# Expert products W1 and W2 from fp16 parts, the weights split on GpSimd during the attention, token rows stored as parts, silu over a whole tile

## What is computed

```python
t = x.reshape(4096, 192); n = layernorm(t)
gate = n @ Wg.T + bg                    # 8 experts
idx = argmax(gate)                      # top 1, so its probability is 1
h = silu(n @ W1[idx].T) * (n @ W2[idx].T)      # W1, W2: 469 x 192
out = t + h @ W3[idx].T                        # W3: 192 x 469
```

## Time and profile before

| | us |
|---|---|
| median of 3 runs | 1055.98 (1052.8 to 1056.65) |
| the profiled execution, its own time | 1051.83 |
| its span, first to last instruction | 1050.0 |
| PE busy | 944.2 |
| DVE busy | 698.3 |
| ACT busy | 631.4 |
| POOL busy | 182.6 |

### The profile page before, as it was taken

How to read it: one execution, slowest core, us unless ns; L and a number is a source line. 1 busy time by engine, 2 the same in 40 slices (tenths; PEclk the granted TensorE clock), 3 DMA queues, 4 the chain that set the end, 5 groups by cost and what they waited for, 6 DMA issues and landing times. The chain is left out here.

```text
span 1050.0 us, 26495 instructions
## 1 busy us (share of the span) xinstructions
PE 944.2 (90%) x8360; PEld 526.3 (50%) x8360; DVE 698.3 (67%) x1074; ACT 631.4 (60%) x1260; POOL 182.6 (17%) x324
## 2 busy tenths in 40 slices
PE   3799958999999999999999999977482999999995
PEld 1566622333333333333333333376481787878784
DVE  6664558999999999999999999335326344434341
ACT  3564416888888888888888888842112343434441
POOL 3340000000000000000000000050301344444442
PEclk9897757999999999999999999987555999999998
DMA  5244762333333333333333332079520111111110
GB/s 148 76 117 161 286 221 60 101 97 96 101 86 98 91 99 94 96 99 89 99 88 99 94 98 80 2 214 240 149 68 19 40 47 52 49 47 57 54 35 2
DMA packets 75791, 101.08 MB, mean 96 GB/s; under 512 B 27747, under 2 KB 44626, under 8 KB 74214
## 3 DMA queue, kind: packets, MB, share of 16 engines
q1 hardware_dynamic: 65012, 80.13, 27.0%
q0 software_dynamic: 10288, 19.76, 6.8%
q10 hardware_dynamic: 450, 0.66, 0.2%
HBM read 72.25 MB, written 30.05 MB: 97 GB/s over the span
## 5 line engine op out<-in xcount | busy, mean ns | idle before, releaser
L804 DVE TENSOR_REDUCE neg_max<-max_ps 128x1 f16<-128x1024 f32 x384 | 452.3, 1222 | 47.0 <-PE max_ps L658 46.5
L787 ACT ACTIVATE probs<-ring_ps 128x512 f32<-128x512 f32 x768 | 413.3, 595 | 64.9 <-PE ring_ps L690 63.4
L690 PE MATMUL ring_ps<-q_side,k_side 113*128 113x512 f16 x768 | 234.1, 386 | 2.0 <-ACT probs L787 1.6
L702 PE MATMUL out_ps<-probs,values 128*32 128x256 f32 x3072 | 205.6, 385 | 0.1
L702 PEld LDWEIGHTS out_ps<-probs,values 128*32 128x32 f32 x3072 | 80.4, 109 | 109.9 <-ACT probs L787 56.2
L658 PE MATMUL max_ps<-k_side,q_side 48*128 48x256 f16 x1536 | 122.8, 279 | 13.4 <-ACT ident L762 7.2
L1383 DVE TENSOR_TENSOR hidden<-hid_ps,silu 118x128 f32<-118x128 f32 (+1 forms) x156 | 45.2, 290 | 108.3 <-ACT silu L1349 108.3
L1349 ACT ACTIVATE silu<-hid_ps 118x128 f32<-118x128 f32 (+1 forms) x156 | 42.5, 273 | 107.7 <-PE hid_ps L1292 107.7
L658 PEld LDWEIGHTS max_ps<-k_side,q_side 48*128 48x128 f16 x1536 | 49.7, 95 | 113.0 <-issue 65.8
L1289 PE MATMUL hid_ps<-slot_t,w_top 128*118 128x128 f32 (+1 forms) x624 | 102.7, 288 | 0.6 <-ACT slot_t L1330 0.6
L690 PEld LDWEIGHTS ring_ps<-q_side,k_side 113*128 113x128 f16 x768 | 51.7, 97 | 99.8 <-ACT probs L787 71.8
(11 more groups left out here) (178 smaller groups left out, 933.1 us busy)
## 6 DMA issues: line engine op xcount, KB each, us to landing
q_side<-rel_split SPq DMA_DIRECT2D x384, 64.0 KB, 2.1
q_side<-qk_split SPq DMA_DIRECT2D x192, 64.0 KB, 2.4
rel_split<-rel_hi SPq DMA_DIRECT2D x6, 1024.0 KB, 4.3
rel_split<-rel_lo SPq DMA_DIRECT2D x6, 1024.0 KB, 6.3
q_side<-qk_split SPq DMA_DIRECT2D x48, 128.0 KB, 2.7
k_side<-qk_split SPq DMA_DIRECT2D x144, 32.0 KB, 1.7
w_top_all<-in_w_t POOLq DMA_DIRECT2D x2, 1876.0 KB, 19.1
qk_split<-att_sb SPq DMA_DIRECT2D x24, 128.0 KB, 2.4
```

Of the source, the lines that this page charges most:

```text
L690: nc.tensor.matmul(ring_ps[turn_of(k) % BANKS][:], k_side[slot(s)][:, tile * P:(tile + 1) * P], q_side[slot(s)][:, tile // 2, (i % 2) * HA ...
L702: last = nc.tensor.matmul(out_ps[quarter * 2 * HD:(quarter + 1) * 2 * HD, :], values[j][:, tile, :], probs[:, u % 2 * GROUP + 2 * i + quar ...
L787: nc.scalar.activation(probs[:, u % 2 * GROUP + i, :], ring_ps[turn_of(k) % BANKS][:], ACT.Exp).then_inc(exp_done, 1)
L804: nc.vector.tensor_reduce(neg_max[:, j % 2, t:t + 1], max_ps[t % 2][:], AX, ALU.max, negate=True).then_inc(tile_max, 1)
```

## The change

- W1, W2 and the normalized tokens are held as two float16 parts, a high one and the rest. In `experts` each product is five fp16 matmuls for each chunk (high x high, high x rest and rest x high for 128 channels; for the other 64, both weight parts against the tokens' high and low part, the tail standing twice in the row), 40 per tile. W3 stays float32.
- PE's step is now: all four chunks with W1, `transposes(n+1)` (four in fp16), all four chunks with W2, `output(n-1)`.
- ACT takes one silu over 512 columns, DVE one product over 512 columns. ACT copies no weights any more; DVE copies `w_top` (1888 fp16 numbers) and `w_tail` (944) first in its step and W3's part last. POOL's program in `experts` is as it was.
- POOL splits the weights in `attention`: four loads before step 0, then a copy and a subtraction in each of steps 3 to 18 (tails), two loads in step 19, a copy and a subtraction in each of steps 24 to 39 (tops). The loop over 48 steps is written out. `load_experts` in `gate` loads W3 only. The position tiles of `project` lie in the buffer that takes the weights afterwards.
- In `gate`, ACT makes the tokens' high part, DVE the rest, POOL doubles the tails, and SP stores 1024 bytes per token in one DMA for each group in place of 768 and 256 in two. The clearing of `slot_rows` moves there from `project`.

The diff, cut:

```diff
-            nc.gpsimd.memset(g.slot_rows[:], 0.0).then_inc(rows_zeroed, 1)
-            pool.wait_ge(rows_zeroed, 1)
...
-            steps(pool, BH, SLOTS, step)
+            done = [0]
+            def split_step(instruction):
+                done[0] += 1
+                instruction.then_inc(split, 1)
+                pool.wait_ge(split, done[0])
+            def split_tail(c):
+                whole = g.weights[:, c * FP:c * FP + F]
+                split_step(nc.gpsimd.tensor_copy(g.w_tail[:, c, 0:F], whole))
+                split_step(nc.gpsimd.tensor_tensor(g.w_tail[TAIL:2 * TAIL, c, 0:F], whole[TAIL:2 * TAIL, :], g.w_tail[TAIL:2 * TAIL, c, 0:F], ALU.subtract))
+            def split_top(c):
+                whole = g.weights[:, (c + 1) * FP:(c + 1) * FP + F]
+                split_step(nc.gpsimd.tensor_copy(g.w_top[:, c, 0, 0:F], whole))
+                split_step(nc.gpsimd.tensor_tensor(g.w_top[:, c, 1, 0:F], whole, g.w_top[:, c, 0, 0:F], ALU.subtract))
+            by_channel = [w.rearrange("e k f -> k e f") for w in (g.w1_t, g.w2_t)]
+            TAILS_FROM, TOPS_FROM = 3, 24
+            for part in range(2):
+                for j in range(2):
+                    pool.wait_ge(g.rel_stored[part][j], 16 * (HEADS // 4))
+            staged = lambda first: g.weights[:, first * FP:(first + 2 * EXPERTS) * FP].rearrange("p (e h f) -> p h e f", h=2, f=FP)[:, :, :, 0:F]
+            for h in range(2):
+                for half in range(2):
+                    pool.dma_start(staged(0)[half * TAIL:(half + 1) * TAIL, h], by_channel[h][P:D]).then_inc(tails_loaded, 16)
+            for n in range(BH):
+                step(Step(n, n // SLOTS, n % SLOTS, BH, True))
+                if n == TAILS_FROM:
+                    pool.wait_ge(tails_loaded, 64)
+                if TAILS_FROM <= n < TAILS_FROM + 2 * EXPERTS:
+                    split_tail(n - TAILS_FROM)
+                if n == TAILS_FROM + 2 * EXPERTS:
+                    for h in range(2):
+                        pool.dma_start(staged(1)[:, h], by_channel[h][0:P]).then_inc(tops_loaded, 16)
+                if n == TOPS_FROM:
+                    pool.wait_ge(tops_loaded, 32)
+                if TOPS_FROM <= n < TOPS_FROM + 2 * EXPERTS:
+                    split_top(n - TOPS_FROM)
+            split_step(nc.gpsimd.memset(g.w_top[:, :, :, F:FP], 0.0))
+            split_step(nc.gpsimd.memset(g.w_tail[:, :, F:FP], 0.0))
...
             def store_normalized(s):
-                sp.wait_ge(tn_ready, TPS * s.n + TPS)
-                rows = g.token_tiles[:, bass.ds(TPS * s.n, TPS), :]
-                sp.dma_start(rows[:, :, 0:D], tn[:, s.slot]).then_inc(tn_stored[s.slot], 16)
-                sp.dma_start(rows[:, :, AT_TAIL:AT_X], tn[:, s.slot, :, P:D]).then_inc(tn_stored[s.slot], 16)
+                sp.wait_ge(tails_doubled, s.n + 1)
+                sp.dma_start(g.token_tiles[:, bass.ds(TPS * s.n, TPS), 0:AT_X],
+                             parts[:, s.slot].rearrange("p t q d -> p t (q d)").bitcast(F32)).then_inc(tn_stored[s.slot], 16)
...
+            nc.gpsimd.memset(g.slot_rows[:], 0.0).then_inc(rows_zeroed, 1)
+            pool.wait_ge(rows_zeroed, 1)
             pool.wait_ge(loaded, 96)
             load_experts(pool, g, experts_loaded)
+            def double_tails(s):
+                pool.wait_ge(tn_hi_done, s.n + 1)
+                pool.wait_ge(tn_lo_done, s.n + 1)
+                nc.gpsimd.tensor_copy(parts[:, s.slot, :, :, D:ROW_PART], parts[:, s.slot, :, :, P:D]).then_inc(tails_doubled, 1)
+            for n in range(STEPS):
+                double_tails(Step(n, n // 2, n % 2, STEPS, True))
+            pool.wait_ge(experts_loaded, 16 * (EXPERTS + 1))
...
+                act.wait_ge(tn_ready, TPS * s.n + TPS)
+                if s.before(2):
+                    act.wait_ge(tn_stored[s.slot], 16 * s.group)
+                nc.scalar.activation(parts[:, s.slot, :, 0, 0:D], tn[:, s.slot], ACT.Copy).then_inc(tn_hi_done, 1)
...
+                dve.wait_ge(tn_hi_done, s.n + 1)
+                nc.vector.tensor_tensor(parts[:, s.slot, :, 1, 0:D], tn[:, s.slot], parts[:, s.slot, :, 0, 0:D], ALU.subtract).then_inc(tn_lo_done, 1)
...
-                for c in range(2):
-                    last = nc.tensor.transpose(t_ps[:, c * FT:(c + 1) * FT], rows[:, j, c * P:(c + 1) * P], g.ident[:])
+                for c in range(4):
+                    last = nc.tensor.transpose(t_ps[:, c * FT:(c + 1) * FT], parts_of(j)[:, c * P:(c + 1) * P], g.ident16[:])
                 last.then_inc(t_ready, 1)
-            def hidden(s, k):
-                j = s.slot
-                at, size = CHUNKS[k]
-                if s.before(1) or k >= 3:
-                    pe.wait_ge(hid_done, NC * s.n + k - 2)
-                out = h_ps[(j + k) % 3]
-                for h in range(2):
-                    nc.tensor.matmul(out[h][0:size, 0:FT], w_top[:, j, h, at:at + size], tt[:, j, 0:FT], start=True, stop=False)
-                for h in range(2):
-                    half = slice(h * TAIL, (h + 1) * TAIL)
-                    last = nc.tensor.matmul(out[h][0:size, 0:FT], w_tail[half, j, at:at + size], tt[half, j, FT:2 * FT],
-                                            start=False, stop=True, tile_position=(h * TAIL, 0))
+            def hidden(j, h):
+                hi_top, hi_tail, lo_top, lo_tail = (tt[:, j, c, :] for c in range(4))
+                for k in range(NC):
+                    some = slice(k * FC, (k + 1) * FC)
+                    out = h_ps[j][h][:, k * FT:(k + 1) * FT]
+                    nc.tensor.matmul(out, w_top[:, j, h, 0, some], hi_top, start=True, stop=False, skip_group_check=True)
+                    nc.tensor.matmul(out, w_top[:, j, h, 0, some], lo_top, start=False, stop=False, skip_group_check=True)
+                    nc.tensor.matmul(out, w_top[:, j, h, 1, some], hi_top, start=False, stop=False, skip_group_check=True)
+                    nc.tensor.matmul(out, w_tail[:, j, h, some], hi_tail, start=False, stop=False, skip_group_check=True)
+                    last = nc.tensor.matmul(out, w_tail[:, j, h, some], lo_tail, start=False, stop=True, skip_group_check=True)
                 last.then_inc(h_ready, 1)
             def output(n, j, reused):
+                pe.wait_ge(hid_done, n + 1)
+                pe.wait_ge(w3_taken, 2 * n + 2)
                 if reused:
                     pe.wait_ge(y_added, n)
                 for k, (at, size) in enumerate(CHUNKS):
-                    pe.wait_ge(hid_done, NC * n + k + 1)
-                for k, (at, size) in enumerate(CHUNKS):
                     last = nc.tensor.matmul(y_ps[:, 0:D], hid[0:size, j, k, :], w3[0:size, j, k, :], start=(k == 0), stop=(k == NC - 1))
                 last.then_inc(y_ready, 1)
...
             def step(s):
                 j = s.slot
                 pe.wait_ge(top_taken, s.n + 1)
-                pe.wait_ge(tail_taken, 3 * s.n + 3)
+                pe.wait_ge(tail_taken, s.n + 1)
                 pe.wait_ge(t_copied, s.n + 1)
-                hidden(s, 0)
+                if s.before(S):
+                    pe.wait_ge(hid_done, s.n - S + 1)
+                hidden(j, 0)
+                if s.after(1):
+                    transposes(s.n + 1, s.group + (j + 1) // S, (j + 1) % S, True)
+                hidden(j, 1)
                 if s.before(1):
                     output(s.n - 1, (j - 1) % S, s.before(2))
-                for k in range(1, NC):
-                    hidden(s, k)
-                    if k == 1 and s.after(1):
-                        transposes(s.n + 1, s.group + (j + 1) // S, (j + 1) % S, True)
             steps(pe, N_T, S, step)
             output(N_T - 1, (N_T - 1) % S, True)
...
-            def take_top(n, j, reused):
...
-            take_top(0, 0, False)
+                    act.wait_ge(h_ready, 2 * (n - S + 1))
+                nc.scalar.activation(tt[:, j].rearrange("p c t -> p (c t)"), t_ps[:, 0:4 * FT], ACT.Copy).then_inc(t_copied, 1)
             copy_t(0, 0, False)
-            take_top(1, 1, False)
             def step(s):
-                for k, (at, size) in enumerate(CHUNKS):
-                    act.wait_ge(h_ready, NC * s.n + k + 1)
-                    if s.before(1) or k >= 2:
-                        act.wait_ge(hid_done, NC * s.n + k - 1)
-                    nc.scalar.activation(act_sb[0:size, k % 2, :], h_ps[(s.slot + k) % 3][0][0:size, 0:FT], ACT.Silu).then_inc(silu_done, 1)
-                    if k == 1 and s.after(1):
-                        copy_t(s.n + 1, (s.slot + 1) % S, s.before(2))
-                if s.after(2):
-                    take_top(s.n + 2, (s.slot + 2) % S, s.before(1))
+                act.wait_ge(h_ready, 2 * s.n + 1)
+                if s.before(S):
+                    act.wait_ge(hid_done, s.n - S + 1)
+                nc.scalar.activation(act_sb[:, s.slot].rearrange("p k t -> p (k t)"), h_ps[s.slot][0][:], ACT.Silu).then_inc(silu_done, 1)
+                if s.after(1):
```

(37 more changed lines are left out.)

63 lines of the change are left out of this document (30 added, 33 removed).

## The result

| | before | after the change |
|---|---|---|
| median | 1054.57 (1052.8 to 1056.65) | **1267.8** (1265.87 to 1270.91) |
| ratio to before, 95% interval | | 1.2024 (1.1987 to 1.206) |
| profiled execution, its span | 1051.83, 1050.0 | 1270.91, 1269.1 |

A forecast was written before the change was run, and what follows sets the result against it. PE's work and a PE-DVE-POOL-gather loop were taken as equally long; 819.1 - 14 + 36 x 11.5 + 5.3 + 10.2 = 1234.6 us span, 1.8 more gives 1236, median 4 above: 1240 us, range 1168 to 1277.

The forecast's parts named there:

- the likeliest case: Experts: PE starts each burst at the low clock, periods 10.9 to 12.45 us, time 1218 to 1274 us; chance 0.61.
- the closed loop: Experts: output(n-1), DVE's residual, POOL's scatter and gather, landing, then transposes(n+2); 6.78 us, as long as PE's work now.
- L: Experts: time from the end of output(n-1) to the start of transposes(n+2); 6.78 us, not shortened by the change.
- The period: Experts: L, then transposes, 20 W2 products and W3; 11.5 us a tile, over 36 periods.
- the burst: Experts: PE's work from the transposes to the end of W3's products; 4.1 to 5.1 us.
- The clock: Experts: PE idle 5.67 us a period, so work restarts at 1.2 GHz, returning to 2.4 GHz during W3.
- The rival with the full clock: Experts: clock stays at 2.4 GHz, period 9.68 us, 1175 us in all; chance 0.24 together with L shorter.
- DVE's copies beside POOL: Experts: DVE's weight copies delay POOL's issues; 0.1 us a period taken, as a rival up to 1.2 us, 1283 us.
- The gate stage: Gate: waits for token stores go and eight groups take 4.98 us each; -14 us, with 0 as the other end.
- The attention: Attention: 32 splits hidden in POOL's 10.2 us waits, loads go where DMA share is 0.34; cost 0, up to 10 allowed.
- the attention longer than now: Sign of a wrong prediction: the attention stage takes longer; POOL or attention held back had chance 0.10, 1262 to 1300 us.
- The rival in which the loop does not set the pace: Experts: gathers ready when PE asks, period 4.2 us, 978 us; needs L below 2.9 us; faster had chance 0.04.

The follow-up runs named there:

- the order alone: Kernel before, with only output(n-1) moved from behind the first chunk to the end of PE's step, all products in float32: 1332.47 us, ratio 1.2673.
- the change without the loop: Changed kernel with five row buffers in place of three, so POOL gathers four tiles ahead, expert steps written out: 1004.9 us, ratio 0.9547.
- the filled kernel: Changed kernel with 60 extra fp16 matmuls in each step behind W1's products, filling PE's wait without changing results: 1220.48 us, ratio 1.1585.
- the control with the steps written out: Changed kernel with the 39 expert steps written out in place of a loop, with no more buffers: 1268.98 us, ratio 1.2027.
- PE's order put back: Changed kernel with output(n-1) moved ahead of the transposes in PE's step, between W1's and W2's products: 1204.94 us, ratio 1.1445.

## Why the prediction was right

The forecast was 1240 us, 1267.8 was measured, and the likeliest case held: the closed loop, with the low clock in each burst. Its steps, one by one:

- **The loop and its order.** Shown from both sides: the order alone costs 279 us in float32, and the change without the loop is faster than before. L was taken as unchanged, 6.78; it is 7.1 in two periods of three and 6.7 in the third, 6.97 on the mean.
- **The period.** 11.5 forecast, 11.84 measured, which is 12 us over 36 periods. The term that was most too small is the burst, taken as 4.6 between bounds of 4.1 and 5.1. It is 5.4 and 4.5 in turn, 5.0 on the mean: in every second period the clock returned only when W3 was done. Part of that lay in a reading. The return of the clock was put 2.6 us after PE began at 50.8 and 4.5 us after 810.0; the rows themselves (0.61 for 53 to 54, 0.53 for 814 to 815) put it near 53.8 and 814.9, that is after 3.0 and 4.9 us. (The fall, put "after some 3 us" of idle time, came 2.1 us after PE's last matmul, at 722.8; no term hangs on it.) The short landings of the last three gathers, taken at 3.3 us like the others in the forecast, gave some 5 us back: 36 periods of 11.97 would have been 17 us above the forecast. That is luck.
- **The clock.** That each burst begins at 1.2 GHz was read from one idle time of 5.55 us and holds. The Trainium skill's page "TensorE: Matmul & The Clock Gate", section "HAM oscillation", has tiles that each wait for a transfer and begin with the clock halved; the trace agrees, at 0.50 after 6.07 us of idle time. The rival with the full clock is nearly what the filled kernel shows: 10.07 us a period against the 9.68 worked out for it.
- **DVE's copies beside POOL.** I took 0.1 us a period. The scatter took 0.4 us longer in two periods of three, 0.3 on the mean. By the Trainium skill's page "SBUF — State Buffer", section "SBUF: two separate sides", POOL's issue would have waited until both copies end, at 1009.28, and with the usual 1.03 us would have ended at 1010.3, 0.86 us late. It ended at 1009.85, 0.4 us late, so the trace does not show it held until both copies end. It does fit a scatter held until the first of them ends: a scatter that the copy of `w_top` preceded ended 0.9 us after that copy's end, whether it had started 0.1 us behind the copy (at 1008.42), 0.2 us behind it (the control with the steps written out) or 0.4 us behind it (at 950.64, with PE's order put back). Whether it waits or is slowed, these rows do not tell.
- **The gate stage.** -14 forecast. The loop over groups ran from 743.58 until about 791, 47.6 us, where it took 58.2 (from 724.95 to 783.1): -11. The waits for stores are gone but one, of 5.78 us, in the third group.
- **The attention.** This step failed: "Cost: 0, hidden by those 10.2 us of POOL's waiting", with 10 us allowed. It cost 19, and "the attention longer than now", one of the prediction's own signs of being wrong, came about. The maxima kept their 1.22 us, and the splits were hidden just as said (a pair takes 0.58 + 1.08 us, the steps stay at 10.8). What I passed over in half a sentence were the loads: "go where the DMA share is 0.34" reads a mean share as room, while what counts is how long a transfer of 8 or 64 KB stands beside one of 938 or 1876 KB.
- **The rest.** The first residual starts at 827.1 where 819.1 - 14 = 805.1 was forecast: +22, the attention's 19 and the gate's 3. The periods add 12, the tail is as forecast, 10.2. Together, rounded, 34.5 us on the span (1234.6 forecast, 1269.1 measured). The median fell 3 us below the profiled execution, where I had added 4: that gives 7 back: 1240 + 34.5 - 7 is the 1267.8 measured, but for rounding.
- **The rival in which the loop does not set the pace** was worked out as 978 us with a period of 4.2. With five buffers the period is 4.33; with 36 x 0.13 = 5 us for that and the attention's and the gate's 22 us on top of 978 one is at 1005, where 1004.9 was measured. The condition for that case was named rightly as well, it only wasn't met by the change.

Of the expectations, the kernel with PE's order put back missed by 110 us: I followed the loop on PE and POOL and not through DVE's list. The filled kernel missed by 10 us, through matmuls that had no wait to fill, and the order alone by 2.5, through the clock.

## What to carry to other kernels

Before making the busiest engine cheaper, look for a closed loop that is just as long: measure it from an engine's output to the wait that this output ends, and lay the new order of every engine's list against it, for what stands between the two ends of the loop is added to it and what stands beside it is free. Where such a loop exists, lengthen its distance (here two more buffers) first; the cheaper work pays only then. Bulk loads that are put beside a busy stage should be cut into pieces and spread over it; here pieces of 117 and 235 KB did no harm beside transfers of 64 KB.
